# A three-layer graph network on one core: edge sums with a node block per tile of edges, and one weight block of the last relational layer composed by VectorE

## The reference

```
# layer 0: messages, sum per node, a GRU cell, a normalisation
m   = relu(concat([h[src], edge_attr]) @ W1.T + b1) @ W2.T + b2
agg = segment_sum(m, dst);  GRU(agg, h) -> h_new;  x = layernorm(x + h + bn(h_new))
# layers 1 and 2: relational, each with 30 basis matrices (512 x 512) and 2 relations
w    = einsum('rb,bio->rio', att, basis)            # w[r] = sum over b of att[r, b] * basis[b]
msg  = sigmoid(x_j @ gate_w[r]) * x_j @ w[r]        # r is the edge's type
out  = segment_sum(msg, row) + x @ root + bias      # relu after the first of the two
result = layernorm(x + out)
```

## Time and profile before

| what | us |
|---|---|
| median of 3 runs | 501.38 (500.28 to 502.05) |
| the profiled execution, its own time | 502.33 |
| its span, first to last instruction | 500.5 |
| PE busy | 469.4 (94%) |
| DVE busy | 296.0 (59%) |
| ACT busy | 205.4 (41%) |
| POOL busy | 105.5 (21%) |

### The profile page before, as it was taken

How to read it: one execution, slowest core, us unless ns; L and a number is a source line. 1 busy time by engine, 2 the same in 40 slices (tenths; PEclk the granted TensorE clock), 3 DMA queues, 4 the chain that set the end, 5 groups by cost and what they waited for, 6 DMA issues and landing times.

```text
span 500.5 us, 6858 instructions
## 1 busy us (share of the span) xinstructions
PE 469.4 (94%) x2310; PEld 316.4 (63%) x2310; DVE 296.0 (59%) x576; ACT 205.4 (41%) x368; POOL 105.5 (21%) x116
## 2 busy tenths in 40 slices
PE   7889987999979899899999999997899999999995
PEld 2334345666646566876756775674566688788884
DVE  5887797799778889565103579866123114542323
ACT  1788873456345443374126122674222004242000
POOL 0000287568766650000000240000000060000000
PEclk9999998899999999999999999999899999999998
DMA  8979678688878871999978799669987550200011
GB/s 252 428 270 411 208 209 272 192 265 258 278 246 269 269 239 45 412 341 379 372 302 296 317 326 359 241 289 369 381 339 283 204 169 1 85 1 1 22 43 42
DMA packets 29639, 121.21 MB, mean 242 GB/s; under 512 B 4330, under 2 KB 7354, under 8 KB 25246
## 3 DMA queue, kind: packets, MB, share of 16 engines
q1 hardware_dynamic: 17950, 92.33, 48.7%
q0 software_dynamic: 7856, 24.91, 16.1%
q10 hardware_dynamic: 3792, 3.43, 2.2%
HBM read 113.85 MB, written 6.82 MB: 241 GB/s over the span
## 4 chain that ended last, share of the span: by engine, by line
PE 66%; DMA 14%; DVE 12%; issue 4%; DVEq 2%; another core or an unknown queue 1%; ACT 0%; SPq 0%
PE ps L1446 13%; DMA basis<-in_basis 13%; PE ps L1501 12%; PE ps L1288 10%; PE ps L1539 9%; PE ps L1324 6%; DVE x L1000 3%; PE ps L1484 3%; PE ps L1372 3%; PE ps L1376 3%; PE ps L1373 2%; DVE rlo L1007 2%; PE ps L1254 1%; DVE X L935 1%
## 5 line engine op out<-in xcount | busy, mean ns | idle before, releaser
L1324 PE MATMUL ps<-xT_lo,xT_hi 128*128 128x512 f32 x237 | 62.6, 407 | 7.9 <-DVE x L1000 6.9
L1288 PE MATMUL ps<-basis,sel 128*32 128x512 f32 x496 | 59.0, 605 | 4.9 <-DMA basis<-in_basis 4.9
L609 POOL DMA_INDIRECT X<-u_rows,esrc x40 | 44.3, 1107 | 77.6 <-DMA u_rows<-X 56.8
L618 POOL DMA_DIRECT2D X<-w_layer x32 | 16.8, 653 | 206.8 <-DMA w_layer<-ev 206.8
L1324 PEld LDWEIGHTS ps<-xT_lo,xT_hi 128*128 128x128 f32 x237 | 42.9, 191 | 25.7 <-DVE x L1000 10.1
L609 POOL DMA_INDIRECT x_sb<-u_rows,esrc x39 | 43.3, 1110 | 18.5 <-issue 9.5
L1539 PE MATMUL ps<-Xr,CT_r 128*128 128x512 f32 x200 | 47.0, 389 | 0.0
L1539 PEld LDWEIGHTS ps<-Xr,CT_r 128*128 128x128 f32 x200 | 37.5, 188 | 7.8
L697 ACT ACTIVATE rhi<-x 128x512 fp32r<-128x512 f32 x60 | 35.5, 630 | 16.9 <-DVE x L1000 13.2
L1159 DVE SCALAR_TENSOR_TENSOR Xr<-ps,gate,Xr 128x512 fp32r<-128x512 f32 x20 | 14.9, 750 | 45.7 <-ACT Xr L796 45.7
L1007 DVE SCALAR_TENSOR_TENSOR rlo<-x,rhi 128x512 fp32r<-128x512 f32 x60 | 39.5, 687 | 0.0
(11 more groups left out here) (232 smaller groups left out, 810.9 us busy)
## 6 DMA issues: line engine op xcount, KB each, us to landing
basis<-in_basis SPq DMA_DIRECT2D x29, 2048.0 KB
X<-in_eaT SPq DMA_DIRECT2D x20, 256.0 KB
basis<-in_basis SPq DMA_DIRECT2D x8, 512.0 KB
X<-w_layer POOLq DMA_DIRECT2D x32, 128.0 KB, 3.0
w_layer<-ev SPq DMA_DIRECT2D x13, 256.0 KB, 10.6
X<-in_WhhT SPq DMA_DIRECT2D x3, 1024.0 KB, 14.9
basis_apart<-in_basis SPq DMA_DIRECT2D x1, 2048.0 KB, 19.0
X<-in_WihT SPq DMA_DIRECT2D x2, 1024.0 KB, 10.1
```

The costliest lines, as they stand in the source:

```text
L609: nc.gpsimd.indirect_dma_start(gat[e % GATHERS], None, t["u"][:, :], bass.IndirectOffsetOnAxis(ap=esrc[:, e:e + 1], axis=0)).then_inc(gat_ ...
L1288: mm = pe.matmul(bank[32 * g:32 * g + 32], sel[:, layer, s], held[:, g, s2], start=(s == 0), stop=(s == 3), tile_position=(0, 32 * g))
L1324: mm = pe.matmul(ps[:, EA_BANKS[s]], part[:, u % 2, s * P:(s + 1) * P], w, start=(i == 0), stop=(i == 2))
```

## The change

**Edge sums.** The first node block of every tile, not of every unit, is packed. `unit_windows` reads one number per unit: the highest count of further blocks among its tiles, and the first block of each of the four. The end nodes in `dstf` are made relative to their tile's first block once, so that the one-hot matrix of a unit needs no register. Further blocks are done for single tiles: where a unit has any, a branch leads DVE and PE through all four tiles; for each tile both read a packed number (`tile_windows`) and branch again, and only a tile with a further block makes a 128 x 128 one-hot (`L1126`) and sums that one tile.

**Weight block.** Layer 2 composes 6 jobs instead of 8 on PE, and the rows that are left, 16 of each 64, 128 in all, are summed by DVE: for each of 30 bases and each relation one `scalar_tensor_tensor` (the first base: `tensor_scalar`) over 128 x 512 numbers, 60 in all (`mix_block`). Rows of the first 14 bases come by 14 transfers of 256 KB on POOL's queue into a ring of three places in `x_sb`, from the moment all rows of x1 are ready; those of the other 16 come on SP's queue into the two basis slots after the last `w` job. `MIX_AFTER` says after which job's extras DVE sums how many. `out` jobs of layer 1 are drained only when 30 sums are done, since they write over the ring. ACT and DVE split the block by itself (`split_block`), and PE waits for it (`block_ready`) before the second layer's first M job of each relation. The rows of h1, of the gate vector and of the second root matrix are put in the block's row order; POOL's loads of composed rows are 8 and 6 transfers instead of 16 and 16, and the second root matrix comes in 16 transfers instead of one.

```diff
-W_AFTER_M = ((1, 1), (1, 4), (0, 3))
+MIX_AFTER = {("M", 0, 0, 1): 2, ("M", 0, 1, 1): 2, ("M", 0, 2, 1): 2, ("M", 0, 3, 1): 2, ("M", 0, 4, 1): 2,
+             ("M", 0, 0, 0): 3, ("M", 0, 1, 0): 3, ("M", 0, 2, 0): 4, ("M", 0, 3, 0): 4, ("M", 0, 4, 0): 16,
+             ("out", 0, 0): 8, ("out", 0, 1): 7, ("out", 0, 2): 5}
+W_AFTER_M = ((1, 1), (1, 4))
+BLOCK_SPLIT_AT = {("out", 0, 3): 1, ("out", 0, 4): 0}
...
-    composed = [("w", layer, tile) for layer in range(2) for tile in range(WT)][EARLY:]
+    composed = [("w", layer, tile) for layer in range(2) for tile in range(TILES[layer])][EARLY:]
...
+        def tile_windows(eng, e):
+            v = eng.value_load(wins[0:1, e:e + 1], min_val=0, max_val=PACK * PACK * NT * ET)
+            return (v % PACK).with_bounds(min_val=0, max_val=NT - 1), (v // PACK % PACK).with_bounds(
+                min_val=0, max_val=NT - 1), v // (PACK * PACK)
...
+                if layer == 0:
+                    pool.wait_ge(x1_ready, NT)
+                    for b in range(RING_BASES):
+                        if b >= RINGS:
+                            pool.wait_ge(mixed, REL * (b - RINGS + 1))
+                        nc.gpsimd.dma_start(ring[b % RINGS], mix_rows(b)).then_inc(ring_in[b % RINGS], 16)
...
-                with dve.If(end > first + 1):
-                    with dve.Fori(first + 1, end) as j:
-                        dve.wait_ge(next_free, j + before + (UNITS - u + 1))
-                        one_hots(oh_next[:], u, j).then_inc(next_ready, 1)
+                with dve.If(extras_here > 0):
+                    for t in range(filled(u)):
+                        e = u * UNIT + t
+                        _, extra, before = tile_windows(dve, e)
+                        with dve.If(extra > 0):
+                            with dve.Fori(1, extra + 1) as d:
+                                dve.wait_ge(next_free, before + d + 1)
+                                dve.tensor_scalar(oh_next[:, t], iota[:, bass.ds(d * P, P)], dstf[:, e:e + 1], None,
+                                                  ALU.is_equal).then_inc(next_ready, 1)
...
+                    if b == 0:
+                        dve.wait_ge(att_all_in, 16)
+                        ins = dve.tensor_scalar(into, rows_of, att_all[:, b, r:r + 1], None, ALU.mult)
+                    else:
+                        ins = nc.vector.scalar_tensor_tensor(out=into, in0=rows_of, scalar=att_all[:, b, r:r + 1],
+                                                             in1=sums_of, op0=ALU.mult, op1=ALU.add)
...
+                with pe.If(extras_here > 0):
+                    for t in range(filled(u)):
+                        first, extra, before = tile_windows(pe, u * UNIT + t)
+                        with pe.If(extra > 0):
+                            with pe.Fori(1, extra + 1) as d:
+                                pe.wait_ge(next_ready, before + d + 1)
+                                tile_sums((first + d).with_bounds(min_val=0, max_val=NT - 1), oh_next[:, t], u, t
+                                          ).then_inc(next_free, 1)
```

More of the change, by code:

```diff
@@ new lines, in _ @@
+                    first_of = sprow[:, 0].rearrange("p (u s) -> p s u", s=UNIT)
+                    sofar = more
+                    for s in range(UNIT - 1, -1, -1):
+                        into = firsts[s % 2] if s else unit_wins
+                        last = nc.vector.scalar_tensor_tensor(out=into, in0=sofar, scalar=float(PACK), in1=first_of[:, s],
+                                                              op0=ALU.mult, op1=ALU.add)
+                        sofar = into
+                        if s:
+                            step(last)
@@ L979, in _ @@
+                    last.then_inc(wins_ready, 1)
                 if w == 2:
```

211 lines of the change are left out of this document (143 added, 68 removed).

## The result

The changed kernel takes 528.36 us (median of four runs, 526.08 to 531.75), the kernel before in the same series 501.72. The ratio is 1.0535, 95% interval 1.0459 to 1.0611: slower by 27 us, and 20 us beyond the upper end of the range. The profiled execution took 531.75 us with a span of 530.0, against 502.33 and 500.5.

A forecast was written before the change was run, and what follows sets the result against it. PE, busy 94% of the span, was taken as the bound, with DVE about equally loaded in the edge sums. Edge sums +4.5 and weight block -2.4 gave +2.1 us on 501.38: 503.5 us, range 497.5 to 508.5.

The forecast's parts named there:

- The edge sums: Whole edge stage: four crossings cost 6.0 us, partly absorbed by late gathers, leaving +4.5 us; bounds -6.0 and +10.
- On PE the same block ends near 99.5 and the fourth tile's pair at 100.4 ... that is no later than DVE, so the two are not added: Crossing unit: PE's reads and branches end no later than DVE's, so they add nothing to DVE's 1.5 us.
- DVE's term: Crossing units: DVE's next add_rows starts 3.1 us later, 1.6 of it slack, so 1.5 us a crossing stays.
- Rival 5: Clock falls behind the gaps at the crossings, or the ring's wait is 5 us: 508 us; chance 0.12.
- hidden: POOL's fewer loads: Weight block: POOL's fewer loads of composed rows cost nothing.
- -7.7, two w jobs removed: Weight block: two w jobs leave PE's path, at 379.31 to 383.4 and 393.81, -7.7 us.
- Basis rows late: PE's wait for basis rows until 350.19: ring loads in flight beside them make it longer, +1.5 us.
- Two sums ahead of the low part: DVE between the drain at 357.50 and the low part at 358.16: two sums lengthen PE's wait, +1.2 us.
- the third base's rows: Those two sums need the third ring load, which probably lands late: +1.8 us, between 0 and 5.
- Hidden: the other 54 sums: DVE in M and out jobs: the sums fit between drains, split ready some 3 us early, cost 0.
- The clock: Weight block: a second PE gap of 3 to 6 us lowers the clock again; half taken, +0.8 us.
- POOL's issue (rival 6): POOL's ring loads starve at issue while DVE sums, +3 us: 506.5 us; chance 0.05.

The follow-up runs named there:

- edges_keep: edges_only with three matmuls of zeros on PE ahead of each of the four reads in a crossing unit: 500.99 us, ratio 1.0212.
- edges_only: The kernel before with the change's edge sums alone, nothing of the weight block: 507.27 us, ratio 1.0334.
- block_only: The kernel before with the change's weight block alone, nothing of the edge sums: 509.76 us, ratio 1.0374.
- edges_pe_one: edges_only, but in a crossing unit PE reads and branches for the crossing tile only, DVE still for all four: 506.41 us, ratio 1.0076.
- Form_of_before: block_order with layer 1's composed rows loaded in the old form and row order, 16 transfers of 128 KB: 517.51 us, ratio 1.0252.
- block_late: block_order, but POOL waits for the last basis rows before the ring's first load: 510.21 us, ratio 1.0366.
- block_order: block_only, but DVE's first sums stand behind relation 1's last M job, none before the last two transposes' low part: 509.15 us, ratio 1.034.
- Ring_fixed: Form_of_before without the 11 later ring loads; DVE sums the first three bases' rows again (wrong numbers): 498.72 us, ratio 0.9882.
- Deep: Form_of_before with no ring: SP issues all 30 transfers of block rows, behind the last w job's basis rows: 508.19 us, ratio 1.0123.
- root_first: Deep with ACT's split later, every third slot transfer on POOL, sums brought forward, eight moved behind relation 0's last M job: 496.11 us, ratio 1.01.

## Why the prediction was wrong

**The edge sums (+4.5, found +12.8): the step that failed is "On PE the same block ends near 99.5 and the fourth tile's pair at 100.4 ... that is no later than DVE, so the two are not added".** PE's path ended last, and not DVE's. On PE 1.1 us a crossing stood against DVE's 1.5. But PE's pair starts 4.3 us behind the unit's last, where 3.5 was forecast (99.5 against 95.99): the block began 0.5 us before that pair instead of 0.9, and it took 4.8 us until the late pair instead of 4.45. With that PE's sums of unit 3 end some 2.0 us later than before, and the late pair starts 2.5 us behind DVE's one-hot. (That PE's reads begin at 97.6 and not near 95 is for 2.1 us the later unit.)

The larger part is the clock, which the prediction held at 1 us a crossing and left to its upper bound: it costs 1.6 (edges_keep). Together that is some 3.5 us a crossing, 14.1 for the four by the traces of edges_only and block_only. DVE's term, 1.5 us a crossing, was good: edges_pe_one has 1.0. The gathers absorbed more than the 1.5 us that I took off, some 3.6 us, and all of it at the third crossing; and 2.2 us stood ahead of the first crossing, which no term had. Rival 5 named the clock, and against it stood that the gap is shorter than 2.72 us; it was 3.25 instead of 2.5.

The Trainium skill gives TensorE's queue 64 entries, in "TensorE: Matmul & The Clock Gate", section "Architectural detail: the array is 16× 32×32, not 1× 128×128". The unit's sums would fit into that, but the trace shows a lead of half a microsecond at the first read, so room in a queue is not a lead.

"Units without a crossing cost nothing" held: the unit from 110.00 to 115.44 takes PE 5.44 us, as in the earlier trace rows.

**The weight block, "hidden: POOL's fewer loads" (0, found some 4 of 5.6).** I counted transfers, 8 instead of 16, and not what each carries. Form_of_before shows the price.

**"-7.7, two w jobs removed."** Right in itself: one compose job follows `("M", 0, 4, 1)`, at 394.16, as in the kernel before, and none comes after it. (The sign "no compose group stands behind" that job was worded wrongly.) PE had this time back only where nothing else waited.

**"Basis rows late" (+1.5).** PE waited 1.03 + 5.27 us instead of 2.72, +3.6. That the ring's loads did it is not shown: with them held back until the basis rows had landed, block_late waited 5.8 us there, more than block_order's 3.1.

**"Two sums ahead of the low part" and "the third base's rows" (+1.2 and +1.8).** The wait was 6.71 us instead of 1.45, +5.3 for a forecast of +3.0, near the upper end. Right in kind: the third base's sums started at 384.71. But block_order shows that mending this alone gains next to nothing. I treated the ring as a matter of its first three loads. It has three places for 14 bases, and each load waits for two sums, POOL and some 9 us of landing, so DVE waited for rows six times, 21.1 us in all.

**"Hidden: the other 54 sums" (0, found some 5).** This is the step of the block that failed most. I counted DVE's time between drains as if rows were always there, at 0.60 us a sum. The sums come every 0.66 us (0.74 shown for one), 3.6 us more for 60, and the first `out` job waited 4.46 us for a drain that stood behind sums without rows. PE waited 0.51 us for the block's split in front of `("M", 1, 0, 1)` as well, which the prediction had named as a sign that it is wrong as a whole. Ring_fixed puts the price of the ring at 13.8 us between the layers. Deep and root_first show what is left even with deeper buffers: the transfers run without a break until PE's own basis rows are in the earlier trace rows, the block's rows then come at 0.20 MB/us, and DVE has 40 us of sums beside its drains, splits and gates.

**The clock (+0.8, found +4.8).** It was at its lower level behind the wait of 6.71 us (0.50, where the earlier trace rows has 0.66), and its mean between the layers 0.90 instead of 0.98. I priced one further gap and took half; PE had three long ones, of 5.27, 6.71 and 4.46 us. So the terms of this part are -7.7 + 3.6 + 5.3 + 4.8, the waits of 4.46 and 0.51 us and 0.2 of ACT's: 11.2, and 11.1 were measured.

**POOL's issue (rival 6)** played no part: the ring's 14 issues took 584 ns in the median and 617 at most, 11 of them between DVE's first sum and its last, where 2.3 us each had been the fear. This row is line L694 of the changed kernel:

```profile
L694 POOL DMA_DIRECT2D x_sb<-in_basis x14: 584/584/617, 363.7 to 417.8; - x14
...
DMA to landing us min/median/max: 3.9/8.8/19.9
```

Left open: what the packets under 512 B are that the new form brings (the bytes of the rows do not need them), what holds SP's queue at 0.20 MB/us for the block's rows, what made PE's basis rows late in the M jobs, and why the block loses less in the changed kernel than alone.

## What to carry to other kernels

When instructions move onto a sequencer, put its start and length on every engine's own path, and give the gap that it opens a price in clock: the same block of reads cost 0.8% on DVE and 2.3% on PE. When work goes to an engine with room, ask first when its data can be there; idle time ahead of the data is no room, and moving waits from one place of the order to another returned nothing here. Count a transfer's packets, not its issues; ask whether data go on flowing behind the last issue before calling the issuing engine the limit; and try each part of a change alone before judging it: of this one, the edge sums with a single read are worth keeping.

## What the chip showed that I had not expected

- A register read with its operations and a branch took 1.1 us on PE's sequencer (reads at 97.6, 98.7, 99.7 and 100.9 us), and four in a row opened 2.9 to 3.3 us of idle time, behind which twelve matmuls took 4.59 us instead of 3.01. Matmuls of zeros in the gap did not make the late pair later and brought 6.3 us back over four crossings.
- One queue with transfers of 256 KB in rows of 2 KB moved 0.20 MB/us with the DMA engines 53% busy, also in the 6 us behind its last issue; basis rows on the same queue move 0.39 MB/us. The issues, 0.63 us each at first, slowed to 1.5 in the mean.
- The other row order of POOL's loads added some 3456 packets under 512 B to 2 MB and 4.7 us of all DMA engines' time.
